# Layer 1's row maxima from products over the 96 rows of the stacked parts, in place of the rank's 32 rows

## The chip, the cores and the metric

The program runs on one core of one Trainium2 chip. The metric is the device time of one execution in microseconds; every comparison is between medians of several runs. TensorE (PE) multiplies, VectorE (DVE) and ScalarE (ACT) drain PSUM and do the elementwise work, GpSimd (POOL) helps, SyncE (SP) issues most of the DMAs.

## The reference

Four layers follow one another on a 1024x256 activation. Each is `x = x + attention(xn) + ffn(xn)` with `xn` the layer norm of `x`. The change lies in the attention of layer 1, whose queries and keys have only 32 features (the rank):

```python
state = jnp.einsum('blh,hr->blr', x, Ws)            # queries, rank 32
action = jnp.einsum('blh,hr->blr', x, Wa)           # keys, rank 32
q_values = jnp.einsum('bir,bjr->bij', state, action) / SCALE
q_values = jnp.where(causal, q_values, -jnp.inf)
weights = jax.nn.softmax(q_values, axis=-1)
out = jnp.einsum('bij,bjh->bih', weights, x)
return jnp.einsum('bih,ho->bio', out, Wo.T) + bo
```

## The kernel before

The kernel is written by hand in one block per engine; each engine goes through its own list in order and waits on counting semaphores. No scheduler changes that order.

Layer 1's attention goes through these steps, in this order on PE:

- The normalised activation is transposed (L1627), and ACT copies it to `xnT` (L872).
- One unit of products with `w_sa` (L1595, `psA<-xnT,Ks`, 64 output rows) gives queries and keys for all 1024 tokens. ACT copies them out five times (L996 to L1000): once whole to `qk1`, and in rounded high parts to rows of `Q1` and `K1`.
- Two units of products with `w_o1` (`value_units`, L1595, `psA<-Ks,xnT`) give the values. ACT copies them to `V1` (L1003). The second unit needs the PSUM buffer that the five copies read.
- DVE makes the two low parts, `qk1` less its high part (L1401 for the queries, L1402 for the keys), and each adds one to `parts1_ready`. After that `Q1` holds high, low, high in rows 0 to 95 and `K1` holds high, high, low, so a product over the 96 rows is high·high + low·high + high·low.
- A softmax needs a bound on each row before it exponentiates. PE makes the scores a first time in bf16 (`MAX1`: 12 units of a 128-query tile against up to 512 keys, L1919, with the mask added by L1922 on the diagonal). `high()` takes the upper two bytes of each word, so these operands are bf16. DVE reduces each unit to a maximum per query (L1405). The units go round four PSUM banks, so PE can be four ahead of DVE.
- PE then does the Hadamard products with `h256` in two units (L1595, `psA<-xnT,Ks`, 128 output rows) with the transpose of the negated maxima (L1669) between them. DVE copies that transpose to `mrow` (L1217) and SP sends it into row 96 of `Q1`.
- PE makes the scores a second time, over 97 rows in full (L1679, mask L1681); ACT exponentiates (L1012); PE multiplies by the values (L1595, `<-Ks,Pr`), and DVE divides and adds to `x` (L1415, L1416, L1419).

The gated feed-forward of layer 1 and two more layers follow.

Of the kernel before, what the change touches and what calls it, by code (L numbers as in the profile page):

```python
# [14 lines left out]
HALF = 512  # L15
# [4 lines left out]
RANK = 32  # L20
# [94 lines left out]
def build(nc, ins, out):  # L115
    with ExitStack() as ctx:
# [7 lines left out]
        def over(base, name, shape, at=0):  # L124

            return nc.alloc_sbuf_tensor_at(name, shape, F32R, offset=offset[base] + 4 * at)

        def sem(name):
            return ctx.enter_context(nc.semaphore(name))
# [57 lines left out]
        Q1, K1 = over("OT", "Q1", [P, T]), over("Ks", "K1", [P, T])  # L187
# [34 lines left out]
        def carve(t):  # L222

            at = [0]

            def part(*dims):
                n = int(np.prod(dims))
                v = t[:, at[0]:at[0] + n]
                at[0] += n
                return v.rearrange("p (a b) -> p a b", a=dims[0]) if len(dims) == 2 else v  # L230
            return part

        part = carve(WA)
# [5 lines left out]
        part = carve(WA)  # L239
# [6 lines left out]
        part = carve(WB)  # L246
        w_up, w_dn, ws_dp = part(DC, INTER), part(FC, D), part(D)
        part = carve(Ks[:, 4 * T:])
        w_gt, h256, w_o1, w_sa = part(DC, INTER), part(DC, D), part(DC, D), part(DC, 2 * RANK)
        bo1 = part(D)  # L250
        part = carve(WB)
        w31, w32, w33 = part(DC, F3), part(DC, F3), part(F3C, D)
        part = carve(W3q)
# [14 lines left out]
        def slot(t, n, rows=P, base=0):  # L268
            return t[base:base + rows, n * T:(n + 1) * T]
# [22 lines left out]
        def tile_cols(j):  # L292
            return slice(j * P, (j + 1) * P)
# [49 lines left out]
        def high(ap):  # L343

            return ap.bitcast(BF16).rearrange("p (t w) -> p t w", w=2)[:, :, 1]
# [99 lines left out]
        parts1_ready, xh_split = sem("parts1_ready"), sem("xh_split")  # L445
# [414 lines left out]
        def _(act):  # L860
# [192 lines left out]
            def cut_piece(m):  # L1053

                if m == E:
                    act.wait_ge(wsu_in, 16)
                for w, _, high_part in piece_sources(m):
                    op = act.activation(high_part, w, ACT.Copy)
                op.then_inc(piece_cut, 1)
# [511 lines left out]
        def _(pe):  # L1571
            na, nd = [0], [0]

            def a_unit():

                na[0] += 1
                if na[0] > 2:
                    pe.wait_ge(a_drained, na[0] - 2)
                return psA[:, (na[0] - 1) % 2, :]

            def d_unit():
                nd[0] += 1
                bank, drained = d_place(nd[0])
                if drained > 0:
                    pe.wait_ge(d_drained, drained)
                return bank
# [5 lines left out]
            def product(dst, terms, start=True, stop=True):  # L1592

                for k, (lhsT, rhs) in enumerate(terms):
                    op = pe.matmul(dst, lhsT, rhs, start=start and k == 0, stop=stop and k == len(terms) - 1)  # L1595
                return op
# [33 lines left out]
            def value_units(lhsT, rhs, chunks, logits=None):  # L1630


                for u in range(2):
                    dst = a_unit()
                    beside_ = d_unit() if logits is not None and u == 0 else None
                    for j in range(4):
                        op = product(dst[:, j * D:(j + 1) * D],
                                     [(lhsT(k, tile_cols(4 * u + j)), rhs(k)) for k in chunks])
                        if beside_ is not None:
                            for jj in (2 * j, 2 * j + 1):  # L1640
                                width = logits.shape[2]
                                last = product(beside_[:, jj * width:(jj + 1) * width],
                                               [(xnT[:, k, tile_cols(jj)], logits[:, k, :]) for k in range(DC)])
                    op.then_inc(a_filled, 1)
                    if beside_ is not None:
                        last.then_inc(d_filled, 1)
# [25 lines left out]
            def scores_T(dst, base, k, q, kt, half, second=None, mask=False):  # L1672

                lo = max(kt * P, half * HALF)
                diagonal = kt * P >= half * HALF
                out_ = dst[:, base + lo - half * HALF:base + HALF]
                if second is not None:
                    pe.matmul(out_, second[0], second[1](lo, (half + 1) * HALF), start=True, stop=False)  # L1678
                op = pe.matmul(out_, k, q(lo, (half + 1) * HALF), start=second is None, stop=not (diagonal and mask))  # L1679
                if diagonal and mask:  # L1680
                    op = pe.matmul(out_[:, 0:P], identb[:], maskk[:], start=False, stop=True)  # L1681
                return op
# [180 lines left out]
            for item in PRE0:  # L1863
# [20 lines left out]
                elif item[0] in ("logits", "router"):  # L1884
# [4 lines left out]
                    if item[0] == "logits":  # L1889
                        j = item[1]  # L1890
# [7 lines left out]
                elif item[0] == "max":  # L1898
# [3 lines left out]
                    j, part, h0, nh, w = item[2]  # L1902
# [10 lines left out]
            features(cols(w_sa, 0, 2 * RANK), normed)  # L1913
            value_units(normed, lambda k: w_o1[:, k, :], range(DC))
            pe.wait_ge(a_drained, A["qk1"])
            for j, part, w in MAX1:
                dst = d_unit()
                diagonal = part == (j >= NT // 2)
                op = pe.matmul(dst[:, 0:w], high(Q1[0:RANK, tile_cols(j)]), high(K1[0:RANK, part * HALF:part * HALF + w]),  # L1919
                               start=True, stop=not diagonal)  # L1920
                if diagonal:
                    op = pe.matmul(dst[:, w - P:w], identb[:], maskq[:], start=False, stop=True)  # L1922
                op.then_inc(d_filled, 1)
# [3 lines left out]
            features(cols(h256, P, 2 * P), normed)  # L1927
            pe.wait_ge(mrow_in, 16 * maxima_of("L1"))
            pe.wait_ge(ones1_ready, 1)
            pe.wait_ge(parts1_ready, 2)  # L1930
            for kt in range(NT):
                dst = a_unit()
                for half in range(2):
                    if kt * P < (half + 1) * HALF:
                        op = scores_T(dst, half * HALF, K1[0:3 * RANK + 1, tile_cols(kt)],
                                      lambda lo, hi: Q1[0:3 * RANK + 1, lo:hi], kt, half, mask=True)
# [3 lines left out]
            for j in range(NT):  # L1940
                dst = d_unit()
# [11 lines left out]
            for u in range(NT // 2):  # L1953
                dst = d_unit()
                for k in range(2):
                    t = tile_cols(2 * u + k)
                    for m in range(FC):
                        if u == k == 0 and (m == 0 or m >= FC - 2):
                            pe.wait_ge(hid1_split, max(m + 1, FC - 2))
                        op = product(dst[:, k * D:(k + 1) * D],  # L1960
                                     [(hid1_high[:, m, t], dn_high[:, m, :]), (hid1_high[:, m, t], dn_low[:, m, :]),
                                      (hid1_low[:, m, t], dn_high[:, m, :])], start=m == 0, stop=m == FC - 1)
# [34 lines left out]
            for u in range(NT // 2):  # L1997
                for terms in (
# [5 lines left out]
                    dst = d_unit()  # L2004
                    for k in range(2):
                        op = product(dst[:, k * D:(k + 1) * D], terms(tile_cols(2 * u + k)))
# [11 lines left out]
            for first, second in ((1, 2), (3, 0)):  # L2018
                for c in range(DC):
                    if first == 1 and c == 0:  # L2020
                        dst = a_unit()
                        for chunks in ((0, 1, 3, 4), (2, 5)):
                            if 2 in chunks:
                                pe.wait_ge(low3_ready, DC)
                            for half in range(2):
                                cs = slice(half * HALF, (half + 1) * HALF)
                                op = product(dst[:, cs], [(w3(first, c)(k), parts3(k, cs)) for k in chunks],
                                             start=0 in chunks, stop=2 in chunks)
# [15 lines left out]
            for u in range(NT // 2):  # L2044
                dst = d_unit()
                for k in range(2):
# [7 lines left out]
                    for c in range(DC):  # L2054
                        op = pe.matmul(dst[:, k * D + c * P:k * D + (c + 1) * P], slot(Qs, 4 + c)[:, t], identf[:],
                                       start=False, stop=c == DC - 1)
# [62 lines left out]
```

## Time and profile before

| | before |
|---|---|
| median of 3 runs | 1012.65 us |
| the three runs | 1007.17, 1012.65, 1013.95 us |
| the profiled execution's own time | 1012.09 us |
| its span (first to last instruction) | 1010.0 us |
| PE busy in the span | 889.0 us |
| mean granted clock of PE | 0.897 |

The profiled execution took 2.1 us more than its span and stands 0.56 us below the median. A granted clock of 1.00 is the upper of TensorE's two levels (2.4 GHz), 0.50 the lower (1.2 GHz); a mean between them is a mixture in time. The three runs of the same program differ by 6.78 us.

### The profile page before, as it was taken

To read this page: it belongs to the slowest core of one execution; us is meant where nothing else is said; L and a number is where in the kernel's file an instruction comes from. 1 tells how busy PE (TensorE), PEld (TensorE's weight loads), DVE (VectorE), ACT (ScalarE), POOL (GpSimd) and SP (SyncE) were. 2 spreads that over 40 slices of the span, in tenths; PEclk is the share of its full clock that TensorE was granted. 3 is DMA by queue.
4 is the path that set the end of the run, shared out by engine and by line. 5 is a ranking of instruction groups with operands and counts; after the bars stand their busy time and mean duration, and the time that the engine had idled before them with its cause. 6 is when DMAs were issued, how large, how long until landed. Compare 5 with 4: busy or idle time off the path is not lost.

```text
span 1010.0 us, 11938 instructions
## 1 busy us (share of the span) xinstructions
PE 889.0 (88%) x4799; PEld 511.0 (51%) x4799; DVE 559.2 (55%) x988; ACT 387.0 (38%) x476; POOL 224.8 (22%) x207
## 2 busy tenths in 40 slices
PE   4998979999999899979589998977999889978997
PEld 2453534344334434424337877623333258778776
DVE  4583566774566367621443355496777426945452
ACT  2503424444443435445441431214556763500340
POOL 2381001323012301342210100400111236610010
PEclk9675999999698969989788998967999989979899
DMA  6675414532921390020400002477100051000001
GB/s 171 132 159 200 63 31 72 119 73 75 156 32 43 94 210 17 1 71 1 146 0 1 1 1 86 107 144 113 17 2 1 1 217 44 1 1 1 1 1 42
DMA packets 35647, 66.81 MB, mean 66 GB/s; under 512 B 5908, under 2 KB 14652, under 8 KB 35524
## 3 DMA queue, kind: packets, MB, share of 16 engines
q1 hardware_dynamic: 35016, 65.92, 28.3%
q8 instruction: 38, 0.62, 0.3%
q10 hardware_dynamic: 576, 0.13, 0.1%
q14 instruction: 17, 0.14, 0.0%
HBM read 45.93 MB, written 16.29 MB: 62 GB/s over the span
## 4 chain that ended last, share of the span: by engine, by line
PE 67%; DVE 19%; ACT 5%; DMA 4%; POOL 2%; issue 2%; SPq 1%; ACTq 0%; DVEq 0%; POOLq 0%
PE psD L1595 12%; PE psA L1595 11%; PE psO L1716 10%; DVE mx L1199 9%; PE psD L1661 9%; PE psO L1595 8%; PE psA L1679 7%; PE psA L1678 3%; DVE hid_low L1509 2%; PE psD L1663 2%; ACT Pr L907 1%; PE psA L1627 1%; DMA Kr<-d_kn 1%; ACT Pr L912 1%; PE psD L1727 1%
## 5 line engine op out<-in xcount | busy, mean ns | idle before, releaser
L1199 DVE TENSOR_REDUCE mx<-psD 128x1 f32<-128x512 f32 (+3 forms) x416 | 259.2, 658 | 127.8 <-PE psD L1663 91.1
L907 ACT ACTIVATE Pr<-psA 128x1024 f32<-128x1024 f32 (+3 forms) x192 | 161.8, 866 | 200.4 <-PE psA L1679 191.0
L776 POOL TENSOR_SCALAR_AFFINE_SELECT Pr<-Pr 128x512 f32<-128x512 f32 x96 | 60.9, 635 | 441.2 <-ACT Pr L907 355.1
L912 ACT ACTIVATE Pr<-psA 128x1024 f32<-128x1024 f32 (+3 forms) x96 | 63.5, 702 | 65.4 <-PE psA L1679 65.0
L1716 PE MATMUL psO<-Pr,Vh 128*32 128x512 f32 (+3 forms) x768 | 82.5, 510 | 3.7 <-POOL Pr L776 3.0
L1678 PE MATMUL psA<-Qr,Kr 128*128 128x512 f32 (+3 forms) x192 | 78.8, 424 | 2.8 <-DMA Qr<-mrow 2.8
L1663 PE MATMUL psD<-maskq,identb 128*128 128x128 bf16 x348 | 73.0, 234 | 0.0
L1679 PE MATMUL psA<-Qr,Kr 113*128 113x512 f32 (+3 forms) x192 | 67.1, 357 | 0.0
L1661 PE MATMUL psD<-Kr,Qr 80*128 80x512 bf16 (+3 forms) x166 | 60.2, 395 | 5.3 <-DVE mx L1199 3.0
L1661 PE MATMUL psD<-Kg,Qs 96*128 96x512 bf16 (+3 forms) x192 | 56.9, 337 | 8.6 <-DVE mx L1199 6.6
L1661 PE MATMUL psD<-Ks,Qs 96*128 96x512 bf16 (+3 forms) x166 | 53.5, 351 | 4.6 <-DVE mx L1199 3.9
L1679 PE MATMUL psA<-Qs,Kg 97*128 97x512 bf16 (+3 forms) x192 | 50.1, 357 | 7.2 <-DMA Qs<-mrowb 4.8
L1679 PE MATMUL psA<-Qs,Ks 97*128 97x512 bf16 (+3 forms) x192 | 45.8, 332 | 5.3 <-ACT Pr L907 3.3
L1678 PEld LDWEIGHTS psA<-Qr,Kr 128*128 128x128 f32 x192 | 37.9, 198 | 18.6 <-ACT Pr L912 6.1
L1661 PEld LDWEIGHTS psD<-Kg,Qs 96*128 96x128 bf16 x192 | 17.9, 97 | 58.0 <-DVE mx L1199 43.1
L1627 PE MATMUL psA<-identf,xn 128*128 128x128 f32 x96 | 21.6, 389 | 27.9 <-DVE xn L1164 27.4
L1661 PEld LDWEIGHTS psD<-Kr,Qr 80*128 80x128 bf16 x166 | 18.3, 111 | 52.0 <-DVE mx L1199 37.0
L1716 PE MATMUL psO<-Pr,Vg 128*32 128x512 f32 (+3 forms) x384 | 41.8, 516 | 1.2 <-POOL Pr L776 0.7
L1661 PEld LDWEIGHTS psD<-Ks,Qs 96*128 96x128 bf16 x166 | 16.5, 101 | 47.3 <-DVE mx L1199 42.4
L1679 PEld LDWEIGHTS psA<-Qr,Kr 113*128 113x128 f32 x192 | 37.9, 198 | 3.9 <-issue 1.7
L1663 PEld LDWEIGHTS psD<-maskq,identb 128*128 128x128 bf16 x348 | 36.7, 106 | 5.7 <-issue 3.2
L1595 PE MATMUL psA<-xnT,WA 128*128 128x512 f32 x56 | 31.3, 720 | 2.7 <-ACT xnT L872 2.2
(402 smaller groups left out, 1684.7 us busy)
## 6 DMA issues: line engine op xcount, KB each, us to landing
Qr<-d_qr SPq DMA_DIRECT2D x18, 512.0 KB, 12.3
d_qr<-WB SPq DMA_DIRECT2D x9, 512.0 KB, 2.6
Pr<-d_cb SPq DMA_DIRECT2D x8, 512.0 KB, 7.1
Qs<-d_gq SPq DMA_DIRECT2D x24, 128.0 KB, 4.7
Qs<-d_q SPq DMA_DIRECT2D x24, 128.0 KB
Ks<-d_k SPq DMA_DIRECT2D x24, 128.0 KB
Qr<-d_qn SPq DMA_DIRECT2D x18, 128.0 KB, 8.3
Kr<-d_kn SPq DMA_DIRECT2D x18, 128.0 KB, 9.2
```

The costliest lines, as they stand in the source:

```text
L776: pool.affine_select(out=block_, in_=block_, pattern=[[0, GH], [1, P]], compare_op=ALU.is_ge, fill=0.0, base=0, channel_multiplier=-1).the ...
L907: act.activation(place[:, h, q0:T], src[:, q0:T], ACT.Exp, scale=score_scale(i)).then_inc(a_drained, 1)
L912: act.activation(place[:, h:h + 2, q0:T], src[:, :, q0 - HALF:HALF], ACT.Exp, scale=score_scale(i)).then_inc(a_drained, 1)
L1199: dve.tensor_reduce(mx[:, j, part, h0:h0 + nh], src, AX, ALU.max).then_inc(d_drained, 1)
L1509: dve.tensor_tensor(hid2_low[:, m - DC, :], slot(Qs, m - DC), hid2_high[:, m - DC, :], ALU.subtract).then_inc(hid2_split, 1)
L1595: op = pe.matmul(dst, lhsT, rhs, start=start and k == 0, stop=stop and k == len(terms) - 1)
L1627: op = pe.transpose(dst[:, tile_cols(j)], src[:, j, c * P:(c + 1) * P], identf[:])
L1661: op = pe.matmul(dst[:, k * w:(k + 1) * w], q, kk, start=True, stop=not diagonal)
L1663: op = pe.matmul(dst[:, (k + 1) * w - P:(k + 1) * w], identb[:], maskq[:], start=False, stop=True)
L1678: pe.matmul(out_, second[0], second[1](lo, (half + 1) * HALF), start=True, stop=False)
L1679: op = pe.matmul(out_, k, q(lo, (half + 1) * HALF), start=second is None, stop=not (diagonal and mask))
L1716: op = pe.matmul(psO[h * VW:(h + 1) * VW, lo:hi], values(i, kt, h), e, start=kt == 0, stop=kt == last_kt, tile_position=(0, h * VW), skip_ ...
```

## The change

The bf16 products from which the maxima come are taken over rows 0 to 95 of `Q1` and `K1` in place of rows 0 to 31. Since rows 32 to 95 hold low parts that DVE makes, the wait for `parts1_ready` moves from ahead of the second scores to ahead of the first product of the maxima. Nothing else changes; the number of instructions on each engine is the same, and so are their output shapes.

```diff
             pe.wait_ge(a_drained, A["qk1"])
+            pe.wait_ge(parts1_ready, 2)
             for j, part, w in MAX1:
                 dst = d_unit()
                 diagonal = part == (j >= NT // 2)
-                op = pe.matmul(dst[:, 0:w], high(Q1[0:RANK, tile_cols(j)]), high(K1[0:RANK, part * HALF:part * HALF + w]),
+                op = pe.matmul(dst[:, 0:w], high(Q1[0:3 * RANK, tile_cols(j)]),
+                               high(K1[0:3 * RANK, part * HALF:part * HALF + w]),
                                start=True, stop=not diagonal)
...
             pe.wait_ge(mrow_in, 16 * maxima_of("L1"))
             pe.wait_ge(ones1_ready, 1)
-            pe.wait_ge(parts1_ready, 2)
             for kt in range(NT):
```

On PE, from the end of the maxima to the second scores, the kernel before has these rows (`Q_56` and `K_57` are `Q1` and `K1`, `had_ready` tells that the weights of the Hadamard products are made):

```order
L1919 MATMUL psO<-K_57,Q_56 128x512 [waits d_drained] x2
L1922 MATMUL psO<-maskq,identb 128x128
L1595 MATMUL psA<-xnT,Ks 128x512 [waits a_drained,had_ready]
L1595 MATMUL psA<-xnT,Ks 128x512 x3
L1669 MATMUL psD<-identf,mneg 8x128 [waits d_drained,max_ready]
L1595 MATMUL psA<-xnT,Ks 128x512 [waits a_drained]
L1595 MATMUL psA<-xnT,Ks 128x512 x3
L1679 MATMUL psA<-Q_56,K_57 128x512 [waits parts1_ready,a_drained,ones1_ready,mrow_in]
```

And these stand there now:

```order
L1920 MATMUL psO<-K_57,Q_56 128x512 [waits d_drained] x2
L1924 MATMUL psO<-maskq,identb 128x128
L1595 MATMUL psA<-xnT,Ks 128x512 [waits a_drained,had_ready]
L1595 MATMUL psA<-xnT,Ks 128x512 x3
L1669 MATMUL psD<-identf,mneg 8x128 [waits d_drained,max_ready]
L1595 MATMUL psA<-xnT,Ks 128x512 [waits a_drained]
L1595 MATMUL psA<-xnT,Ks 128x512 x3
L1679 MATMUL psA<-Q_56,K_57 128x512 [waits a_drained,ones1_ready,mrow_in]
```

No instruction has moved: only the wait has gone from the last row, and it stands now on the first product of the maxima, seventeen instructions earlier than the first row above.

## Rows read from the trace of the kernel before

**Rows 1.** The page: busy time by engine, and PE's clock in 40 slices.
```profile
PE 889.0 (88%) x4799; PEld 511.0 (51%) x4799; DVE 559.2 (55%) x988; ACT 387.0 (38%) x476; POOL 224.8 (22%) x207
...
PEclk9675999999698969989788998967999989979899
```

**Rows 2.** Stretches of layer 1's attention: length, busy PE, PEld, DVE, ACT, POOL, clock, DMA.
```profile
499.10:509.40 10.30, 8.87 (x36) 6.19 (x34) 2.43 (x2) 5.99 (x6) 0.00 (x0) 1.00 0.00 0
509.40:512.80 3.40, 3.25 (x17) 1.42 (x16) 2.85 (x7) 2.82 (x2) 0.37 (x1) 1.00 0.00 0
512.80:519.60 6.80, 6.80 (x12) 2.51 (x11) 3.21 (x7) 0.00 (x0) 4.28 (x2) 0.50 0.00 0
519.60:526.30 6.70, 5.97 (x18) 2.51 (x16) 0.28 (x1) 3.06 (x4) 0.00 (x0) 1.00 0.00 1
526.30:529.80 3.50, 0.12 (x1) 0.12 (x1) 2.36 (x2) 3.47 (x5) 0.00 (x0) 1.00 0.00 0
529.80:540.10 10.30, 9.76 (x27) 6.91 (x28) 2.15 (x6) 5.18 (x8) 0.00 (x0) 0.50 0.00 1
```

**Rows 3.** Timeline around the start of the maxima: start, length, engine, line, what.
```profile
504.71 1.01 ACT L1000 ACTIVATE Q<-psA 32x1024 fp32r<-32x1024 f32 x1
...
505.76 1.22 DVE L1401 TENSOR_TENSOR Q<-gate,Q 32x1024 fp32r<-32x1024 f32 x1 [12.75 <-ACT Q L1000]
...
505.78 3.72 PE L1595 MATMUL psA<-Ks,xnT 128*128 128x256 f32 x16 [1.43 <-ACT Q L1000]
507.00 1.22 DVE L1402 TENSOR_TENSOR K<-gate,K 32x1024 fp32r<-32x1024 f32 x1
...
509.43 0.23 PE L1919 MATMUL psD<-K,Q 32*128 32x128 bf16 x1
```

**Rows 4.** The chain that ended last, in order of time, over the maxima and the Hadamard products.
```profile
513.44 0.96 PE psO L1919 x2
514.41 0.22 PE psO L1922
514.62 6.02 PE psA L1595 x8
520.65 0.11 PE psD L1669
520.75 3.45 PE psA L1595 x8
```

**Rows 5.** Timeline of DVE, PE and SP from the last maxima to the second scores.
```profile
514.55 1.27 DVE L1405 TENSOR_REDUCE mx<-psO 128x1 f32<-128x512 f32 x2
...
515.86 0.18 DVE L1204 TENSOR_REDUCE mneg<-mx 128x8 f32<-128x16 f32 x1
...
520.89 0.28 DVE L1217 CAST mrow<-psD 8x128 fp32r<-8x128 f32 x1 [4.85 <-PE psD L1669]
...
521.20 0.78 SPq L483 DMA_DIRECT2D Q<-mrow  x1
...
523.63 0.79 PE L1679 MATMUL psA<-Q,K 97*128 97x512 f32 x1
```

**Rows 6.** PE's groups by shape, maxima of layer 1, 509.4 to 512.4 us.
```profile
L1919 PE MATMUL psO<-K,Q 32*128 32x512 bf16 x2 | 0.8, 396 | 0.0
...
L1919 PE MATMUL psO<-K,Q 32*128 32x384 bf16 x1 | 0.3, 338 | 0.0
```

**Rows 7.** PE's groups by shape, 132 to 154 us: maxima over 96 rows in layer 0.
```profile
L1661 PE MATMUL psD<-Kg,Qs 96*128 96x512 bf16 x18 | 6.7, 388 | 3.4 <-DVE mx L1199 3.3
...
L1661 PE MATMUL psD<-Kg,Qs 96*128 96x384 bf16 x8 | 2.5, 334 | 1.0 <-DVE mx L1199 0.9
```

**Rows 8.** Four stretches of layer 0, columns as in rows 2.
```profile
65.60:89.50 23.90, 23.90 (x57) 10.77 (x56) 15.53 (x26) 4.82 (x12) 11.86 (x7) 0.50 0.68 159
132.00:154.30 22.30, 17.29 (x111) 7.73 (x110) 19.04 (x32) 4.34 (x6) 1.27 (x2) 1.00 0.19 36
154.40:157.80 3.40, 2.34 (x15) 0.73 (x12) 3.00 (x5) 0.00 (x0) 0.00 (x0) 1.00 0.00 0
157.80:161.20 3.40, 3.40 (x14) 2.45 (x16) 1.30 (x4) 1.56 (x2) 0.00 (x0) 0.50 0.00 0
```

**Rows 9.** PE's costliest groups by shape between 65.6 and 89.5 us.
```profile
L1595 PE MATMUL psA<-OT,WA 64*128 64x512 f32 x8 | 7.6, 1096 | 0.0
L1595 PE MATMUL psA<-WA,OT 64*128 64x256 f32 x16 | 7.2, 641 | 0.0
```

**Rows 10.** Timeline of PE over the first products with the values.
```profile
534.79 1.23 PE L1595 MATMUL psD<-Ks,Pr 128*128 128x257 f32 x2 [0.37 <-ACT Pr L1012]
535.81 4.44 PE L1595 MATMUL psO<-Ks,Pr 128*128 128x257 f32 x10
540.09 4.08 PE L1595 MATMUL psD<-Ks,Pr 128*128 128x257 f32 x18
```

## The prediction

> **What bounds the kernel now.** I read the page first. PE is busy for 88% of the span and the other engines for 55% at most, so PE sets the pace nearly everywhere; the row of its clock shows slices of 9 and slices of 5 to 7, so part of that pace is the clock [rows 1]. Then the stretches around the change. PE runs at 1.00 through the value products, goes on at 1.00 through most of the maxima, falls to 0.50 at 512.8 us, comes back at 519.6, falls again at 529.8 after a stretch in which it did almost nothing, and is back at 540.1 [rows 2]. The fall at 512.8 is the odd one. PE was busy for 3.25 of the 3.40 us ahead of it. What it did there were products over 32 rows and masks. The chain of waits shows what the fall costs: the chain lies on PE from the last two products of the maxima through both Hadamard units to the second scores [rows 4], and the first Hadamard unit lies whole in the slow stretch. DVE reduces without a pause up to 515.82 [rows 5], but PE is past its last product by 514.6 and waits for none of this.
>
> **Part 1, the wait that moves.** The first product of the maxima now needs both low parts. The second value unit on PE and DVE's first subtraction are released by the same copy (L1000), at 505.78 and 505.76 [rows 3]. DVE's two subtractions take 1.22 us each and end at 508.22. PE reaches the maxima at 509.43, so 1.21 us later. The cover is the value unit of 3.65 us, which ran at the full clock and can't be shorter. Cost 0. Behind the waiting instruction all of PE's list would stand, and DVE's reductions with it; were the cover gone, the cost would be 2.44 us, the two subtractions. At the old place the wait had been over for 15 us (508.22 against 523.63 [rows 5]), so its removal there gives 0.
>
> **Part 2, three times the rows in twelve products.** A product streams the same columns whether 32 or 96 rows take part. The bf16 product of 32x512 took 396 ns and that of 32x384 338 ns [rows 6]; the products of 96x512 took 388 ns and those of 96x384 334 ns, at the same clock of 1.00 [rows 7, 8]. Twelve times -8 ns is -0.1 us at one end, and DVE paces the later units anyway, so 0 is the value I take and -0.1 to 0 the bounds. DVE's twelve reductions read results of the same shape: 0. The maxima come out closer to the true scores, and nothing depends on them in time.
>
> **Part 3, the clock.** Here the rows of the trace say that a product over few rows keeps the clock less well than its busy time suggests. From 65.6 to 89.5 us PE was busy for all 23.9 us and the clock stayed at 0.50 throughout [rows 8]; the costliest groups were products over 64 rows [rows 9]. Against this, from 132.0 to 154.3 us PE was busy for only 17.3 of 22.3 us, much of it with maxima over 96 rows, and the clock stayed at 1.00 [rows 7, 8]. Directly behind it PE was busy for 2.34 of 3.40 us and the clock fell [rows 8]. So 69% busy with 96 rows and more fell, 78% held, and 96% busy with 32 rows fell [rows 2]. The changed stretch is 96% busy with 96 rows. It lies nearer to the one that held. It is not as safe as it looks, since the units of the maxima are short and paced by DVE towards their end, and a busy time in bf16 products of this size counts the latency of each.
>
> If the clock holds, the first Hadamard unit, 6.02 us in the chain, takes what the second takes at (nearly) full clock, 3.45 us [rows 4]: a gain of 2.57 us. The last products of the maxima, 0.96 us of which lie in the chain at half clock, would shrink by up to half, 0.48 us, but their start waits for DVE to free a bank, which doesn't get faster; 0 to 0.48, and I take 0. What is late next: the transpose of the maxima needs L1204, done at 516.04, while the unit ahead of it would end at 514.62 + 3.45 = 518.07, so it does not wait. The row's way from there to the second scores (cast at 520.89, DMA issued at 521.20, scores at 523.63 [rows 5]) starts at the same transpose and moves with it. ACT's copies of the Hadamard units move too, and the chain of copies, exponentials and scores behind them is the same work. So the 2.57 us arrive at the value products.
>
> What follows them depends on when the clock falls and comes back during the idle stretch at 526.3. Of the 10.3 us at 0.50 behind it [rows 2], 5.3 us are value products, twelve instructions at 0.44 us each against 0.227 for one at full clock [rows 10]. Moved by 2.57 us, this slow stretch may cover none of them or more of them: from -12 x 0.217 = -2.6 us to, for one more stretch of 3.4 us such as [rows 8] show, 15 x 0.217 = +3.3 us. The row that I take is the one that stands there, 0.
>
> **Sum.** 0 (wait) + 0 (rows) - 2.6 (first Hadamard unit) + 0 (later slow stretch) = -2.6 us. Against the profiled execution's own 1012.09 us (span 1010.0, 2.1 us around it) this gives 1009.5; it stood 0.56 us below the median, so the median becomes 1012.65 - 2.6 = **1010.0 us**.
>
> The Trainium skill speaks against this sum. Its page "TensorE: Matmul & The Clock Gate", section "What's actually happening", says that the clock is set by how busy the PE has been recently, and the section "Why this matters for your kernels" that a single product over 32 rows takes the same time as one over 128. By the second the trace agrees (396 against 388 ns). By the first, read as busy time alone, rows would not matter, the same fall would come at the same place, and the sum would be 0; the stretch from 65.6 us, all busy and at half clock, speaks against that reading.
>
> **The rivals.**
>
> A, the forecast: the clock holds through the maxima, or comes back before most of the first Hadamard unit is done. With the bounds above (-0.1, -0.5) alone it gives 1009.4 to 1010.1; where it falls and comes back early, half of the term, 1011.4. Chance 0.48.
>
> B, rows don't matter to the clock, or matter too little for these short units; the change then does not do what it could. PE's products take as long as before, the wait is hidden, and the time is 1012.65 us. For it speaks that the fall behind 154.4 came in spite of 96 rows. Chance 0.32.
>
> C, the clock holds, and the slow stretch behind the idle time also ends before the value products begin: -2.6 - 2.6 = -5.2 us, 1007.4. Chance 0.10.
>
> D, slower. The mechanism is the clock's return after the idle stretch at 526.3. It costs as soon as it comes later than 5.3 us after the first value product (534.79 against 540.1 now). PE arrives there earlier than before if A's gain is had, so that with an unlucky return up to 15 more value products run at half clock: +3.3 us. If A's gain is not had as well, the time is 1012.65 + 3.3 = 1016.0. For it speaks that such slow stretches of 6.8 and 10.3 us stand in the same rows; against it, that nothing in the change moves them this way. Chance 0.08.
>
> E, slower by the wait: DVE's subtractions end more than 1.21 us later than now, at most +2.4 us, 1015.1. Both sides start from one copy, so I see no reason for it. Chance 0.02.
>
> **How the numbers follow.** The likeliest case gives 1010.0. The program's own three runs lie between 1007.17 and 1013.95, and a median of such runs can lie some 2.5 us to either side of its centre, which counts more than most terms here. A and C with this scatter reach down to about 1006, B with part of it up to 1014; D and E in full lie beyond and are what I leave out. Range 1006.0 to 1014.0. One per cent, which is 10.1 us and about what a measurement of this kernel can tell from no change, is more than any case gives: -5.2 is 0.5% faster, +3.3 is 0.3% slower. To be over 1% faster, some 20 us at half clock would have to vanish. So within 1%: 0.94; faster by over 1%: 0.03; slower by over 1%: 0.03, these two for something that I don't see.
>
> **What would show it.** In the changed kernel's profile the stretch from the value products to the second Hadamard unit should stand at clock 1.00 (A), or show 0.50 beginning within the maxima as now (B). The first Hadamard unit, eight instructions, should take some 3.5 us and no longer 6. The first product of the maxima should start directly behind the value unit, with no idle time released by DVE's L1402. The products of 96x512 should last 390 to 400 ns at clock 1.00. The DVE reductions should last as long as now. The prediction is wrong if the clock falls in the same place in spite of the 96 rows, or if idle time stands ahead of the first product of the maxima.

## The result, and the profile after

Over 20 runs each, the changed kernel took 1003.56 us in the median and the kernel before 1007.45 us. The medians lie 3.9 us apart. The ratio is 0.9958 with a 95% interval of 0.9939 to 0.9977, which makes 4.2 us faster, between 2.3 and 6.1 us. The profiled execution took 1004.49 us with a span of 1002.4 us and a mean clock of 0.905. The three runs of the kernel before that the prediction had to go by had a median of 1012.65 us; seventeen more runs put it 5.2 us lower.

The chain that ended last in the changed kernel, in order of time, as [rows 4] of before (start, length, engine, what, instructions):

```profile
501.09 3.72 PE psA L1595 x16
...
504.81 0.06 PE psD L1920
504.87 0.07 PE psD L1924
...
504.97 3.08 DVE mx L1405 x7
...
508.10 0.73 PE psO L1920 x2
508.83 0.06 PE psO L1924
508.89 3.49 PE psA L1595 x8
512.38 0.11 PE psD L1669
512.49 3.45 PE psA L1595 x8
```

The first Hadamard unit takes 3.49 us in place of 6.02, as long as the second. The last two products of the maxima and their mask take 0.79 us in place of 1.18. The first two pieces are 0.06 and 0.07 us; more of that below.

The stretches of the changed kernel, which answer to [rows 2] (length, busy PE, PEld, DVE, ACT, POOL with counts, clock, DMA share, GB/s):

```profile
495.90:504.60 8.70, 7.27 (x33) 6.01 (x33) 2.43 (x2) 5.98 (x6) 0.00 (x0) 1.00 0.00 0
504.60:508.70 4.10, 3.35 (x21) 1.47 (x20) 3.73 (x9) 2.82 (x2) 0.95 (x1) 1.00 0.00 0
508.70:512.30 3.60, 3.60 (x11) 1.58 (x10) 2.12 (x5) 0.00 (x0) 3.60 (x2) 1.00 0.00 0
512.30:515.40 3.10, 3.10 (x11) 1.43 (x9) 0.28 (x1) 1.02 (x1) 0.11 (x1) 1.00 0.01 1
515.40:518.80 3.40, 1.92 (x8) 0.73 (x6) 0.69 (x1) 2.81 (x3) 0.00 (x0) 0.99 0.00 0
518.80:532.40 13.60, 10.37 (x28) 7.47 (x29) 3.99 (x9) 7.78 (x11) 0.00 (x0) 0.50 0.00 1
```

The clock stays at 1.00 from the value products to the second scores, with PE busy for 82% of the maxima; before, it fell behind a stretch that was 96% busy. It falls at 518.8 us, 1 us into the stretch in which PE waits for ACT, where before it fell at the end of that stretch [rows 2]. The slow stretch is therefore 13.6 us long in place of 10.3, and the first value products still run at half clock.

The start of the maxima in the changed kernel (timeline of PE: start, length of a record, shape):

```profile
504.65 0.22 PE L1920 MATMUL psD<-K,Q 96*128 96x128 bf16 x1
504.71 0.22 PE L1924 MATMUL psD<-maskq,identb 128*128 128x128 bf16 x1
504.77 0.28 PE L1920 MATMUL psD<-K,Q 96*128 96x256 bf16 x1
504.89 0.22 PE L1924 MATMUL psD<-maskq,identb 128*128 128x128 bf16 x1
```

And in another execution of the kernel before (experiment 11), where PE reached them at the same clock:

```profile
502.06 0.23 PE L1919 MATMUL psD<-K,Q 32*128 32x128 bf16 x1
502.22 0.23 PE L1922 MATMUL psD<-maskq,identb 128*128 128x128 bf16 x1
502.38 0.28 PE L1919 MATMUL psD<-K,Q 32*128 32x256 bf16 x1
502.60 0.23 PE L1922 MATMUL psD<-maskq,identb 128*128 128x128 bf16 x1
```

The records are as long in both (0.22 and 0.23 us), and this is what the prediction compared. The starts are not: a product over 32 rows of 128 columns and the mask over 128 rows start 0.16 us apart, one over 96 rows and the mask 0.06. Records of 0.22 us whose starts are 0.06 us apart overlap, so what a product costs a busy PE is not its record's length but the distance to the next start. A second thing has changed beside the clock: a pause of 0.10 us at each step between 32 and 128 rows is gone.

### The profile page after: what moved, and what is told of

It reads as the page before. It is cut to its first block, busy times and chain, and to the rows that moved or that the text cites. A ratio compares the mean times of both kernels' runs of the same rounds, so it can differ in the third digit from the quotient of the medians.

```text
span 1002.4 us, 11937 instructions
## 1 busy us (share of the span) xinstructions
PE 878.3 (88%) x4799; PEld 507.1 (51%) x4799; DVE 556.0 (55%) x988; ACT 386.8 (39%) x476; POOL 224.8 (22%) x207
## 4 chain that ended last, share of the span: by engine, by line
PE 65%; DVE 20%; ACT 6%; DMA 5%; POOL 2%; issue 2%; SPq 1%; ACTq 0%; DVEq 0%; POOLq 0%
PE psD L1595 11%; PE psA L1595 11%; PE psO L1716 10%; DVE mx L1199 9%; PE psD L1661 9%; PE psA L1679 8%; PE psO L1595 7%; PE psA L1678 3%; DVE hid_low L1509 2%; PE psD L1663 2%; DMA Kr<-d_kn 1%; ACT Pr L907 1%; PE psA L1627 1%; ACT Pr L912 1%; SPq L483 1%
## 5 line engine op out<-in xcount | busy, mean ns | idle before, releaser
L1661 PE MATMUL psD<-Ks,Qs 96*128 96x512 bf16 (+3 forms) x166 | 56.3, 371 | 3.9 <-DVE mx L1199 3.2
L1678 PEld LDWEIGHTS psA<-Qr,Kr 128*128 128x128 f32 x192 | 37.7, 196 | 18.3 <-ACT Pr L912 6.4
```

Of the source, the lines that this page charges most:

```text
L1661: op = pe.matmul(dst[:, k * w:(k + 1) * w], q, kk, start=True, stop=not diagonal)
```

## The experiments

Two questions were open. What keeps the clock: the rows, the wait's place, or chance? And what is the pause? Each row comes from one profiled execution where it doesn't say two, and each kernel was timed beside the kernel before on the same chip where a ratio is given. The chips differ between experiments, so kernels are compared with each other by their ratios. A "step" is a change between a product over 32 or 64 rows and one over 96 or 128, the way into the maxima and out of them counted. "Section" is the time from the first product of the maxima to the first Hadamard product, "unit" the first Hadamard unit in the chain.

| | rows of the products | steps | section us | unit us | ratio to before, 95% interval |
|---|---|---|---|---|---|
| before, two executions | 32 | 16 | 4.99, 4.92 | 6.02, 6.29 | 1 |
| changed | 96 | none | 4.08 | 3.49 | 0.9958, 0.9939 to 0.9977 |
| e1 | 32, wait moved | 16 | 4.91 | 6.29 | 0.9996, 0.9981 to 1.0011 |
| e2 | 64, wait moved | 16 | 4.92 | 6.22 | 1.0022, 1.0004 to 1.0040 |
| e3 | 128 | none | 4.06 | 3.49 | 0.9974, 0.9958 to 0.9991 |
| e4 | 32 and filler over 128 | 24 | 8.25 | 6.01 | 1.0039, 1.0023 to 1.0056 |
| e5 | 32, masks too | 2 | 4.42 | 5.01 | 1.0002, 0.9989 to 1.0016 |
| e6, e12 (two executions) | 96, and 32 in added ones | 24 | 5.00, 5.63 | 3.49, 5.93 | 1.0002, 0.9980 to 1.0023 |
| e9 | 96, of which 64 zeros | none | 4.07 | 3.49 | 0.9983, 0.9956 to 1.0011 |

**Experiment 1, the moved wait alone.**

```diff
-                op = pe.matmul(dst[:, 0:w], high(Q1[0:3 * RANK, tile_cols(j)]),
-                               high(K1[0:3 * RANK, part * HALF:part * HALF + w]),
+                op = pe.matmul(dst[:, 0:w], high(Q1[0:RANK, tile_cols(j)]),
+                               high(K1[0:RANK, part * HALF:part * HALF + w]),
```

> The moved wait alone, the products stay over 32 rows. Rows theory (the rows that take part in a product count for PE's clock): as the kernel before, ratio 1.000, clock falls to 0.50 within or behind the maxima and the first Hadamard unit takes about 6 us, 3.6 us only where the clock came back early. Theory of the wait (the gain comes from where the wait stands): as the changed kernel, ratio 0.996, first Hadamard unit 3.65 us. Theory of chance (the clock's fall there differs from execution to execution whatever the kernel): either, and the ratio 1.000.

The time is that of the kernel before, and so is the profile. The wait neither costs nor gives anything; the gain is in the rows.

**Experiment 2, 64 rows.** The same edit with `2 * RANK`.

> The products of the maxima over 64 rows, wait moved. Rows theory: between the two kernels, clock falls in most executions as with 32 rows, ratio 0.997 to 1.000, first Hadamard unit 5 to 6.2 us. Theory that any low part or the moved wait does it: as the changed kernel, ratio 0.996.

64 rows behave as 32 do: 0.16 us between a product of 128 columns and the mask, section and unit as before, and the clock falls. The rows theory expected 64 rows to lie between the two kernels, and they don't; the ratio is, if anything, above 1.

**Experiment 3, 128 rows.** The same edit with `4 * RANK`, the wait for the two memsets added, and

```diff
-link(dve.memset(K1[3 * RANK:3 * RANK + 1, :].bitcast(F32), 1.0))
+link(dve.memset(Q1[3 * RANK:P, :].bitcast(F32), 0.0))
+link(dve.memset(K1[3 * RANK:P, :].bitcast(F32), 1.0))
```

> The products of the maxima over all 128 rows, the last 32 of them zeros in the queries' tile and ones in the keys'. The values are those of the changed kernel; two memsets of 32 rows, about 0.9 us each on DVE while it waits for the copies anyway. Rows theory: the clock stays at 1.00 through the maxima at least as surely as with 96 rows, first Hadamard unit 3.65 us, ratio to the kernel before 0.995 to 0.996. Theory that the values that stream count, not the rows that are addressed: no further gain, zeros add nothing. Theory of chance: ratio 1.000.

The profile is that of the changed kernel to 0.02 us in section and unit. The ratio, 0.9974, lies a little above the changed kernel's and above the 0.995 to 0.996 that were expected, and the intervals overlap.

**Experiment 4, the old rows with filler.**

```diff
+if j >= NT // 2:
+    pe.matmul(dst[:, 0:w], identb[:], high(xnT[:, 0, 0:w]), start=True, stop=True)
 op = pe.matmul(dst[:, 0:w], high(Q1[0:RANK, tile_cols(j)]), ...
```

> The kernel before (32 rows, wait at its old place) with eight more products over 128 rows ahead of the units of the last four query tiles, in the same bank, overwritten by the unit itself; they add 3328 columns. PE waits for DVE in these units, so their own time is hidden. Theory that rows times columns keep the clock: clock 1.00 through the maxima, first Hadamard unit 3.65 us, ratio 0.996 to 0.997, although no product of the maxima has more rows. Theory that the moved wait or the 96 rows' precision does it: ratio 1.000 or above, up to 1.002 for the added products.

This miss showed the pause. The timeline of PE, experiment 4:

```profile
504.41 0.23 PE L1920 MATMUL psD<-xnT,identb 128*128 128x128 bf16 x1
...
504.57 0.23 PE L1921 MATMUL psD<-K,Q 32*128 32x128 bf16 x1
504.73 0.23 PE L1924 MATMUL psD<-maskq,identb 128*128 128x128 bf16 x1
504.80 0.39 PE L1920 MATMUL psO<-xnT,identb 128*128 128x512 bf16 x1
505.12 0.41 PE L1921 MATMUL psO<-K,Q 32*128 32x512 bf16 x1
```

From the filler (128 rows) to the product (32) to the mask (128) the starts are 0.16 us apart each; from the mask to the next filler, both over 128 rows, 0.07. The eight filler products made 24 steps of 16: a filler between two products over 32 rows adds two, one behind a mask none. PE was no longer ahead of DVE, the section grew from 4.9 to 8.25 us, and the clock fell in it in spite of 3328 more columns. Most of the growth is the filler itself, much of it at half clock (0.43 us from the filler of 384 columns to the next product, 0.54 to 0.56 us from those of 512); the pauses add to it. Products that were meant to be free under DVE weren't.

**Experiment 5, 32 rows without steps.**

```diff
-op = pe.matmul(dst[:, w - P:w], identb[:], maskq[:], start=False, stop=True)
+op = pe.matmul(dst[:, w - P:w], identb[0:RANK, :], maskq[0:RANK, :], start=False, stop=True)
```

> The changed kernel with all products of the maxima back on 32 rows, the mask's too: it takes the first 32 rows of the mask alone, so that the causal mask is left out for three quarters of the queries in the diagonal blocks (the maxima are then still upper bounds of those of the kept scores). The columns are the same, and no product has another row count than its neighbour. Theory R (the rows of a product count for the clock): fewer rows than ever, the clock falls within the maxima, first Hadamard unit 6.2 us, ratio to the kernel before 1.000. Theory S (going from a product over 32 or 64 rows to one over 128 and back leaves a pause of some 0.1 us on PE each time, and these pauses are what lets the clock fall): first products 0.06 and 0.12 us apart in place of 0.16 and 0.22, the clock stays at 1.00, first Hadamard unit 3.65 us, ratio 0.996.

The timeline and the stretches of experiment 5:

```profile
503.58 0.23 PE L1920 MATMUL psD<-K,Q 32*128 32x128 bf16 x1
503.65 0.21 PE L1924 MATMUL psD<-maskq,identb 32*128 32x128 bf16 x1
503.70 0.27 PE L1920 MATMUL psD<-K,Q 32*128 32x256 bf16 x1
503.82 0.21 PE L1924 MATMUL psD<-maskq,identb 32*128 32x128 bf16 x1
```
```profile
503.60:507.40 3.80, 2.99 (x20) 1.26 (x20) 3.50 (x9) 2.82 (x2) 0.82 (x1) 1.00 0.00 0
507.40:510.80 3.40, 3.40 (x7) 1.34 (x7) 2.35 (x5) 0.00 (x0) 3.40 (x2) 0.50 0.00 0
```

Each theory is half right. The pause is gone between the products though all are over 32 rows, so it belongs to the step and not to the few rows. The clock falls all the same, for 3.4 us here, so it does not need the pauses to fall. PE was busy for 79% of the stretch ahead of the fall, against 82% in the changed kernel, which held; so small a difference in busy time is a weaker candidate than a fourth to a third of the rows. This experiment alone doesn't exclude it, but the kernel before fell at 96%, so more busy time didn't keep the clock there. The section is 4.42 us: of the 0.84 to 0.91 us that the changed kernel gains in it, 0.5 to 0.6 come from the pauses between the products. The other 0.34 are the clock at its end together with the step out of the 32 rows, which is still there (0.24 us from the last mask to the Hadamard product, 0.08 in the kernel before, both at half clock). From the first product of the maxima to the end of the value products this execution takes 41.2 us, 2.3 to 2.6 less than those of the kernel before (43.5 and 43.8). The ratio of 1.0002 (0.9989 to 1.0016) doesn't show them, and why is open: other executions may have the longer fall.

**Experiments 6 and 12, 96 rows with steps added, two executions.**

```diff
+pe.matmul(dst[:, 0:8], high(Q1[0:RANK, tile_cols(j)]), high(K1[0:RANK, 0:8]), start=True, stop=True)
 op = pe.matmul(dst[:, 0:w], high(Q1[0:3 * RANK, tile_cols(j)]), ...
```

> The changed kernel (96 rows) with one more product over 32 rows and 8 columns ahead of each of the twelve units, overwritten by the unit: 24 more changes of the row count, 96 more columns. Theory R: clock 1.00 through the maxima, first Hadamard unit 3.65 us, ratio 0.996 to 0.997. Theory S: each unit takes some 0.2 us longer, the clock falls within the maxima, first Hadamard unit about 6 us, ratio 1.000 to 1.001.

> A second look at the kernel with 96 rows and 24 added changes of the row count, whose ratio of 1.000 does not fit the clock of 1.00 that its first profile showed. If its clock is a matter of where the maxima lie in the execution: the clock falls here, first Hadamard unit 5 to 6 us. If 96 rows keep it surely: 1.00 and 3.65 us again, and the ratio is from elsewhere.

The timeline of PE, experiment 12, and the stretches of experiments 6 and 12:

```profile
504.90 0.17 PE L1920 MATMUL psD<-K,Q 32*128 32x8 bf16 x1
505.01 0.23 PE L1921 MATMUL psD<-K,Q 96*128 96x128 bf16 x1
505.08 0.22 PE L1925 MATMUL psD<-maskq,identb 128*128 128x128 bf16 x1
505.23 0.18 PE L1920 MATMUL psD<-K,Q 32*128 32x8 bf16 x1
```
```profile
502.30:507.30 5.00, 5.00 (x34) 2.47 (x33) 4.49 (x10) 2.82 (x2) 2.04 (x1) 1.00 0.00 0
```
```profile
504.90:508.70 3.80, 3.80 (x26) 1.90 (x25) 3.25 (x8) 2.82 (x2) 0.80 (x1) 1.00 0.00 0
508.70:515.50 6.80, 6.80 (x14) 2.78 (x14) 2.92 (x7) 0.00 (x0) 3.85 (x2) 0.50 0.00 0
```

A product of 8 columns costs 0.11 us ahead of one over 96 rows, and the mask ahead of it stands 0.15 us off in place of 0.06. From 96 to 128 rows there is no pause (0.07 us): 96 rows count as 128 here. The section is 0.92 us longer with the clock at 1.00. And the clock held in one execution and fell in the other, from the same kernel. With 96 rows but pauses and products over 32 rows between them it can go either way, which is compatible with the ratio of 1.000: the time of the changed kernel plus 0.9 us, and in some executions the slow unit as well. Which of the two added things lets the clock fall isn't separated. The two executions also differ in where the clock had risen ahead of the maxima, 13.9 us before the first product in experiment 6 and 13.3 us in experiment 12; whether that decides it, no run tells. "Surely", as theory R had it, is wrong.

**Experiment 9, rows of zeros.** The maxima's operands are copies in idle buffers, rows 32 to 95 zero:

```diff
+link(dve.memset(Kz, 0.0))
+link(dve.memset(Qz, 0.0))
 dve.wait_ge(a_drained, A["qk1"])
+dve.tensor_copy(Qz[0:RANK, :], high(Q1[0:RANK, :])).then_inc(zero_rows, 1)
+dve.tensor_copy(Kz[0:RANK, :], high(K1[0:RANK, :])).then_inc(zero_rows, 1)
```

> The maxima from products that address 96 rows, of which rows 32 to 95 hold zeros in both operands: copies of the high parts and zeros in buffers that are idle here. The values are those of the kernel before, the shape of the products is that of the changed one. DVE makes two copies of 32 rows (at most 1.2 us each) before the low parts, under the value unit of 3.65 us. If the rows addressed set both the pause and the clock: as the changed kernel, first products 0.06 and 0.12 us apart, clock 1.00 through the maxima, first Hadamard unit 3.65 us, ratio 0.996. If the clock wants rows in which values stream: no pauses, but the clock falls within the maxima, first Hadamard unit 5 to 6.2 us, ratio 0.998 to 1.000.

The stretches of experiment 9, over the maxima and over the first Hadamard unit:

```profile
505.10:509.20 4.10, 3.28 (x22) 1.48 (x20) 4.05 (x10) 2.82 (x2) 1.01 (x1) 1.00 0.00 0
509.20:512.70 3.50, 3.50 (x11) 1.48 (x10) 2.05 (x5) 0.00 (x0) 3.50 (x2) 1.00 0.00 0
```

The maxima are those of the kernel before, the shapes those of the changed one, and the profile is the changed one's. What the rows hold doesn't matter for the pause or, in this execution, for the clock; that they are addressed does. The ratio of 0.9983 was expected at 0.996; its interval holds both 0.996 and 1, so the timing alone would not have told.

**Experiment 7, the same pause at another place.** Layer 0's rotary products alternate between 128 and 64 rows.

```diff
-dve.tensor_tensor(wq_low[0:LAT, :], WA[0:LAT, 2 * DC * P:2 * DC * P + 2 * T], wq_high[0:LAT, :],
+dve.tensor_tensor(wq_low[:], WA[:, 2 * DC * P:2 * DC * P + 2 * T], wq_high[:],
...
-                                   (wq_low[0:LAT, tile_cols(m)], lat_parts[0:LAT, c])]).then_inc(d_filled, 1)
+                                   (wq_low[:, tile_cols(m)], lat_parts[:, c])]).then_inc(d_filled, 1)
```

> The changed kernel with another place of the same kind mended: layer 0's rotary products alternate between 128 rows (high part of the weights) and 64 rows (low part). Here the low part is made and multiplied over 128 rows too, which adds the product of the two low parts, nothing else. There are 64 such products, 32 of them in a row before the first maxima, each 0.43 us at clock 1.00 and 0.72 at 0.50. Theory S, for the pause: 0.22 to 0.25 us at 1.00; if the clock stays up, 32 products take 8 us in place of 20, ratio to the kernel before down to 0.985, less where another engine or a transfer is late next (0.990). Theory R: no pause to win, the products stay at 0.43 and 0.72 us, but more rows may keep the clock up: 0.990 to 0.996. If neither holds: 0.996 as the changed kernel.

The timeline of PE, first of the kernel before, then of experiment 7:

```profile
31.56 0.50 PE L1595 MATMUL psO<-lat_parts,wq_low 64*128 64x512 f32 x1
31.99 0.49 PE L1595 MATMUL psO<-lat_parts,wq_high 128*128 128x512 f32 x1
...
37.16 0.79 PE L1595 MATMUL psD<-lat_parts,wq_high 128*128 128x512 f32 x1
37.88 0.79 PE L1595 MATMUL psD<-lat_parts,wq_low 64*128 64x512 f32 x1
```
```profile
29.86 0.39 PE L1595 MATMUL psO<-lat_parts,wq_low 128*128 128x512 f32 x1
30.09 0.40 PE L1595 MATMUL psO<-lat_parts,wq_high 128*128 128x512 f32 x1
...
39.36 0.39 PE L1595 MATMUL psD<-lat_parts,wq_low 128*128 128x512 f32 x1
48.16 0.27 PE L1661 MATMUL psO<-Kr,Qr 80*128 80x128 bf16 x1 [8.41 <-DMA Kr<-d_kn]
```

The starts of the first eight products come 0.23 us apart in place of 0.43 at the full clock (0.72 at half), as theory S had it; from the ninth on PE is held up by DVE, and the mean is 0.32. The 32 products take 10.2 us at clock 1.00. The 20.5 us that they took in the first profile of the kernel before are mostly half clock. In experiment 11, the same kernel at full clock there, the same place reads:

```profile
27.94 0.50 PE L1595 MATMUL psO<-lat_parts,wq_high 128*128 128x512 f32 x1
...
46.52 0.27 PE L1661 MATMUL psO<-Kr,Qr 80*128 80x128 bf16 x1 [4.84 <-DMA Kr<-d_kn]
```

PE is done sooner in experiment 7 and stands still for 8.4 us in place of 4.8 until keys arrive by DMA, the wait that theory S left room for. From the first rotary product to the one behind that wait it takes 18.6 us in both (18.7 in the changed kernel). So the pauses that are gone here give nothing: the DMA is what is late. The other 32 rotary products lie in later groups with no such wait; there four of them take 0.93 us to the next product in place of 1.60, and all 32 together 11.2 us in place of the changed kernel's 14.9, some of it clock. The ratio to the kernel before is 0.9929, 0.9901 to 0.9957. That overlaps the changed kernel's 0.9939 to 0.9977, so the times don't show that this edit adds to the change.

**Experiment 8, filler that makes no steps.** Where PE waits for ACT between the second and the third unit of the second scores:

```diff
+if kt == 1:
+    spare, drained = d_place(nd[0] + 1)
+    pe.wait_ge(d_drained, drained)
+    for _ in range(12):
+        pe.matmul(spare, high(Q1[0:3 * RANK, 0:P]), high(K1[0:3 * RANK, 0:HALF]), start=True, stop=True)
```

> The changed kernel with twelve products over 96 rows and 512 columns, thrown away, behind the second unit of layer 1's second scores, where PE waits 3.6 us for ACT. They end before ACT is done. If the idle stretch is what lets the clock fall at 518.8 us, it now holds through the first products with the values (5.3 us at half speed before): scores to values as now, the first twelve value products 2.7 us in place of 5.3, ratio to the kernel before 0.993. If the clock does not count such products, or falls elsewhere, ratio 0.996.

The stretches of experiment 8:

```profile
517.60:521.30 3.70, 2.94 (x13) 1.10 (x12) 2.36 (x2) 3.67 (x5) 0.00 (x0) 1.00 0.00 0
521.30:525.00 3.70, 3.21 (x14) 1.86 (x14) 0.00 (x0) 3.59 (x7) 0.00 (x0) 1.00 0.00 0
525.00:528.40 3.40, 3.03 (x9) 2.30 (x9) 1.08 (x3) 1.71 (x3) 0.00 (x0) 0.50 0.00 0
```

The clock holds through the idle stretch, falls only at 525.0 and is back at 528.4. From the first product of the maxima to the end of the value products it takes 37.9 us against 40.4 in the changed kernel. The ratio, 0.9972, 0.9953 to 0.9991, doesn't show these 2.5 us beside the changed kernel's 0.9958; the rest of the profiled execution behind the value products is 0.8 us longer, and where the remainder went stays open.

**Experiment 10, 7 and 8 together.**

> The changed kernel with the rotary products over 128 rows and the twelve products that are thrown away in the scores' idle stretch, both at once. If the two add up: 0.9929 less what the fill gives, 1.5 to 2.6 us, ratio 0.990 to 0.992. If a clock kept here only falls elsewhere: 0.993.

0.9911, 0.9877 to 0.9944, 998.84 us in the median of six runs: faster than the kernel before, and probably than the changed one, whose interval it overlaps from 0.9939 to 0.9944. How much of it is the filler's can't be told from 0.9929.

**Experiment 11, the kernel before once more.**

> A second look at the kernel before. Rows theory: clock falls within the maxima again, maxima section (first product to first Hadamard product) 4.9 to 5.0 us, first Hadamard unit 5 to 6.2 us. Theory of chance: 3.65 us in some looks.

Its stretches, with the rotary products in the first two:

```profile
31.50:45.10 13.60, 10.18 (x24) 4.29 (x24) 9.29 (x14) 8.91 (x10) 11.82 (x6) 1.00 0.89 181
45.10:51.90 6.80, 5.38 (x20) 3.29 (x21) 1.97 (x3) 0.82 (x1) 6.80 (x4) 0.50 1.02 217
...
502.00:505.90 3.90, 3.71 (x18) 1.52 (x17) 3.32 (x8) 2.82 (x2) 0.83 (x1) 0.99 0.00 0
505.90:512.70 6.80, 6.77 (x10) 2.75 (x11) 2.74 (x6) 0.00 (x0) 3.81 (x2) 0.50 0.00 0
```

The fall within the maxima is there again, so it is no chance: both executions of the kernel before, and experiments 1, 2, 4 and 5, have it; the changed kernel and experiments 3, 7, 8, 9 and 10, with 96 rows or more and no steps, have not. Nor is it where the maxima happen to lie against the clock's last rise: that rise comes 13.2 us before their first product in the changed kernel and experiments 3 and 10, which held, and 13.2 to 13.3 in experiments 1, 5 and 11, which fell; it comes 10.3 us before in experiment 7, which held, and in the first profile of the kernel before, which fell. Elsewhere the same program differs. The clock was at 1.00 through the rotary products until 45.1 us here, and at 0.50 from 34.9 to 55.4 in the trace that the prediction read. This execution took 1005.25 us, the other 1012.09.

## Why the prediction was right and where it was wrong

**The wait** (0): right. The first product starts directly behind the value unit, and experiment 1 gives 0.9996 for the wait alone.

**The clock and the first Hadamard unit** (-2.6 us, case A): right in mechanism and size. The clock held, and the unit went from 6.02 to 3.49 us, where the forecast said 3.45. One reading was loose: the unit did not lie whole in the slow stretch, which ended at 519.6 while the unit ended at 520.65, and the other execution of the kernel before has 6.29 us. Experiments 1, 2, 3, 5 and 9 show that the addressed rows do it. The Trainium skill, "TensorE: Matmul & The Clock Gate", section "What's actually happening", has the clock follow how busy PE was recently. Read as busy time alone, it would have kept the fall, and the trace disagrees: the clock fell behind 96% busy before and held at 82% after.

**Three times the rows in twelve products** (0, with -0.1 to 0 as bounds): mis-sized, since the step compared the lengths of records (396 against 388 ns) and not the distances of starts. The last products, taken at 0 of 0 to 0.48, belong to the same stretch. Both terms together are the section, which went from 4.92 to 4.99 down to 4.08 us: -0.8 to -0.9. The step into the maxima, 0.31 us from the last value product in place of 0.22, is another -0.1 ahead of it. The Trainium skill has a drain that may be this pause, in "TensorEngine Tiling (Array Packing)", section "Key Properties": changing the tiling mode drains TensorE. The trace fits, with 0.16 against 0.06 us, if a product over 32 or 64 rows is such a change although the program never asks for a tile; that the pause is this drain, no run shows.

**The later slow stretch** (0, between -2.6 and +3.3): nearly right. The first twelve value products take 5.5 us in the chain, at half clock as before. The clock comes back 5.8 us after the first of them in place of 5.3, and all value products take 18.4 us in place of 18.2 and 18.3 in the two executions of the kernel before.

With the mis-sized terms put right the sum is -2.5 - 0.9 = -3.4 us; from the first product of the maxima to the first value product the profiles have 25.36 and 21.95 us. The measured -4.2 us (-3.9 by the medians) has -3.4, and -3.5 with the step into the maxima, in its interval. The rest may be noise or a later clock; no run here tells.

**The time** (1010.0, range 1006.0 to 1014.0): wrong, the changed kernel takes 1003.56. The step that failed is the base. The prediction gave the median of three runs a scatter of 2.5 us; it lay 5.2 us above the median of 20. From 1007.45 the forecast of -2.6 would have been 1004.9. So of the 6.4 us by which the time was missed, 5.2 are the base and 0.8 to 0.9 the mis-sized terms. The traces say where such scatter is from: the profiled execution of before had 6.8 us more than experiment 11's, with a mean clock of 0.897 against 0.906. It is spread over several slow stretches; the rotary products at half clock, with the wait behind them, make 1.9 us of it (20.5 against 18.6).

**The rivals.** B (rows don't matter, 1012.65) is refuted by the changed kernel against experiment 1, and by experiments 3 and 9. Of C and D, the later stretch ending sooner or later, the changed kernel's profile shows D at a tenth of its size, 0.1 to 0.3 us; experiment 8 shows that most of C's gain can be brought about (value products 17.0 us in place of 18.4, the slow stretch ending 2.9 us after the first of them). E, the exposed wait, did not happen.

## What to carry to other kernels

Read what a product costs from the distance between starts, not from a record's length, and look for products over 64 rows or fewer between ones over 128: each step cost PE 0.1 us in bf16 here and 0.2 us in the rotary products, and went away where 96 or 128 rows were addressed, zeros included in one case. It is time gained only where PE is what is late: ahead of the wait for keys it gave nothing. Judge whether PE keeps its clock by the rows that its products address as well as by how busy it is. Before an absolute time is forecast from a few runs of a program whose clock comes and goes, look at where its slow stretches fall; the difference is safer than the level.

## What the runs showed of the hardware that was not expected

- A step between a product over 32 or 64 rows and one over 128 costs 0.10 us between starts in bf16 at the full clock (0.16 against 0.06 us at 128 columns). Between 96 and 128 rows there is none (0.06 to 0.07 us), nor between 32 and 32 (0.07).
- In the rotary products the same step costs 0.20 us at the full clock (0.43 against 0.23) and 0.72 us stood between starts at half clock.
- Rows of zeros keep the clock at 1.00 in the same place where 32 rows without them let it fall.
- The clock at one place can differ between two executions of one kernel (experiments 6 and 12: unit 3.49 and 5.93 us).
